# Layer 0: GpSimd joins the pair sums of sizes in twos, and TensorE sums once for four key tiles

## What is computed

```python
q = rotate(xn @ Wq.T); k = rotate(xn @ Wk.T * 32 ** -0.5); v = xn @ Wv.T      # xn: group norm of x
qk = einsum('bhqd,bhkd->bhqk', q, k) * mask[None]                              # decay by distance
den = clip(abs(qk).sum(-1, keepdims=True), 1.0, 50000.0)
out = einsum('bhqk,bhkd->bhqd', qk / den, v)
out = gelu((out - mean) / sqrt(var + 1e-5) * ln_g + ln_b) @ Wo.T;  x = x + out
```

## Time and profile before

| | us |
|---|---|
| median of 3 runs | 3395.98 (3387.21 to 3409.24) |
| the profiled execution, its span | 3401.5 |
| TensorE busy, whole span | 3075.4 |
| VectorE busy | 2193.4 |
| ScalarE busy | 2038.7 |
| GpSimd busy | 1165.8 |

### The profile page before, as it was taken

The page is one execution under the profiler, slowest core; times in us unless marked ns, Lnnn a source line. Parts: engine busy times, 40 slices in busy tenths (PEclk is TensorE's granted clock), DMA queues, the critical chain, the costliest instruction groups (busy, mean ns, idle before and its releaser), DMA issues. The chain is left out here.

```text
span 3401.5 us, 94014 instructions
## 1 busy us (share of the span) xinstructions
PE 3075.4 (90%) x38656; PEld 1731.0 (51%) x38656; DVE 2193.4 (64%) x5202; ACT 2038.7 (60%) x4412; POOL 1165.8 (34%) x1446
## 2 busy tenths in 40 slices
PE   6999999999975999999999877999995889999996
PEld 2333333333313656565555545777774566666664
DVE  5878878877753667767676643554554566666664
ACT  2667666766653555555655524566663677777774
POOL 3433434433311222122122202222222465555554
PEclk9999999999996999999999988999998999999998
DMA  6777788687763333233332214445444233333332
GB/s 203 159 173 158 164 178 182 140 184 160 150 141 107 67 88 78 67 82 80 85 73 76 73 41 163 141 149 163 148 134 154 62 93 115 112 117 114 114 98 80
DMA packets 299401, 413.96 MB, mean 122 GB/s; under 512 B 39120, under 2 KB 255968, under 8 KB 277984
## 3 DMA queue, kind: packets, MB, share of 16 engines
q1 hardware_dynamic: 275664, 272.15, 26.8%
q0 software_dynamic: 18432, 134.23, 19.8%
q10 hardware_dynamic: 4880, 1.57, 0.2%
HBM read 219.32 MB, written 53.81 MB: 80 GB/s over the span
## 5 line engine op out<-in xcount | busy, mean ns | idle before, releaser
L732 DVE TENSOR_TENSOR l_probs<-l_psum,l_decay 128x1024 f32<-128x1024 f32 x512 | 598.5, 1218 | 162.0 <-PE l_psum L628 149.6
L780 ACT ACTIVATE l_sizes<-l_probs 128x2048 f32<-128x2048 f32 x256 | 487.0, 1908 | 296.7 <-DVE l_probs L732 291.4
L1806 ACT ACTIVATE l_logits<-l_logits,l_low 128x100 f32<-128x100 f32 x1024 | 372.7, 366 | 205.9 <-DVE l_low L1786 205.0
L1813 POOL TENSOR_TENSOR l_logits<-l_logits,l_inv 128x400 f32<-128x400 f32 x256 | 234.7, 917 | 691.0 <-DVE l_inv L1792 686.6
L628 PE MATMUL l_psum<-l_qk 32*128 32x512 f32 x2048 | 338.4, 641 | 7.9 <-POOL l_qk L866 4.2
L881 POOL DMA_DIRECT2D l_sizes<-l_sizes x128 | 111.2, 869 | 548.1 <-ACT l_sizes L780 536.1
L1643 POOL TENSOR_TENSOR l_E<-l_E,l_causal 128x1024 f32<-128x1024 f32 x64 | 153.0, 2391 | 389.9 <-DVE l_x_act L1341 233.2
L643 PE MATMUL l_psum<-l_probs,l_V 128*32 128x512 f32 x2048 | 270.6, 600 | 1.8 <-DVE l_probs L732 1.6
L2753 POOL TENSOR_SCALAR l_soft<-l_dist,l_sharp,l_border 128x100 f32<-128x100 f32 x512 | 243.6, 497 | 0.1
L299 PE MATMUL l_psum<-l_xT,l_w_up 128*128 128x512 f32 x512 | 230.4, 603 | 13.2 <-DVE l_row_var L1399 13.1
L1748 PE MATMUL l_psum<-l_keys,l_q_blocks 128*64 128x100 f32 x4096 | 230.0, 253 | 3.9 <-issue 2.3
(11 more groups left out here) (247 smaller groups left out, 6085.1 us busy)
## 6 DMA issues: line engine op xcount, KB each, us to landing
l_sizes<-l_sizes POOLq DMA_DIRECT2D x128, 1024.0 KB, 7.5
l_V_windows<-v_image SPq DMA_DIRECT2D x512, 100.0 KB
l_V_windows<-v_padded SPq DMA_DIRECT2D x512, 100.0 KB
l_E<-rows_c SPq DMA_DIRECT2D x64, 512.0 KB, 5.9
l_xT<-y SPq DMA_DIRECT2D x24, 1024.0 KB, 5.2
y<-l_res SPq DMA_DIRECT2D x32, 512.0 KB, 3.2
l_e_everywhere<-rows_e SPq DMA_DIRECT2D x112, 128.0 KB, 5.7
l_xT<-x SPq DMA_DIRECT2D x8, 1024.0 KB, 10.8
```

The lines of the kernel that those rows point to most:

```text
L732: nc.vector.tensor_tensor(probs[:, N % 2, 2 * p:2 * p + 2, :], ring.region(name).rearrange("p (a n) -> p a n", a=2), decay[:, h:h + 2, s0: ...
L780: nc.scalar.activation(sizes[:, slot(N), :, :], probs[:, N % 2, :, :], ACT.Abs).then_inc(sized, 1)
L1806: nc.scalar.activation(e, e, ACT.Exp, scale=-1.0, bias=self.low[:, N % 4, i:i + 1], accum_out=self.total[:, N % 4, i:i + 1]).then_inc(self ...
L1813: nc.gpsimd.tensor_tensor(p, p, self.inv[:, N % 4, :].unsqueeze(2).to_broadcast([P, STEP, NKEY]), ALU.mult).then_inc(self.p_ready, 1)
```

## The change

Sizes are still added in pairs by transfers, but GpSimd now adds two pair sums into one (`join_pairs(f)`, a 128 x 2048 addition, f = N // 4), and TensorE sums once for each four steps: 64 groups of four products instead of 128. The sum of f stands after scores(4f + 8). `sizes` has six buffers instead of five (four for even steps, two for odd), and `swapped`, which the rotation uses, one instead of two. A join stands on GpSimd behind the add_pair of step 4f + 5, that is at n = 1, 5, 9 and 13. The fills now stand at the same steps for both g: q at 3, var at 5, k at 7, v at 11; `out` and `gn` stay. GpSimd's rotations stand at 3 and 7, `normalise` at 7, `inverse` at 6, `gelu` at 8, `values` at 11; the group norm's variance stays at 9 and its `apply` goes to 11. Line numbers of the new kernel are two or three lower (L650 is the sum, L878 the transfer, L884 the join).

```diff
@@ layer0_fill
-    late = 2 * g
-    names = {1 + late: [("q", H + 1)], 3 + late: [("k", H + 1)], 5 + late: [("var", H - 1)], 7 + late: [("v", H + 1)]}.get(n, [])
+    names = {3: [("q", H + 1)], 5: [("var", H - 1)], 7: [("k", H + 1)], 11: [("v", H + 1)]}.get(n, [])
...
-        sw = L.sb("swapped", [P, 2, T])
+        sw = L.sb("swapped", [P, T])
...
-        sizes = L.sb("sizes", [P, 5, 4, BANK])
+        sizes = L.sb("sizes", [P, 6, 4, BANK])
...
-            return N // 2 % 3 if N % 2 == 0 else 3 + N // 2 % 2
+            return N // 2 % 4 if N % 2 == 0 else 4 + N // 2 % 2
...
@@ TensorE
-                def add_sizes(p):
-                    pair_added(pe, p)
-                    if p % PAIRS == 0 and p > 0:
-                        pe.wait_ge(d_copied, p // PAIRS)
+                def add_sizes(f):
+                    pe.wait_ge(joined, f + 1)
+                    if f % FOURS == 0 and f > 0:
+                        pe.wait_ge(d_copied, f // FOURS)
                     for a in range(4):
-                        i = nc.tensor.matmul(PS[a * HD:(a + 1) * HD, 7 * BANK:8 * BANK], ones[:, :], sizes[:, slot(2 * p), a, :],
-                                             start=(p % PAIRS == 0), stop=(p % PAIRS == PAIRS - 1))
+                        i = nc.tensor.matmul(PS[a * HD:(a + 1) * HD, 7 * BANK:8 * BANK], ones[:, :], sizes[:, slot(4 * f + 2), a, :],
+                                             start=(f % FOURS == 0), stop=(f % FOURS == FOURS - 1))
...
-                        if n % 2 == 0 and N // 2 >= LATE:
-                            add_sizes(N // 2 - LATE)
+                        if n % 4 == 0 and N >= 8:
+                            add_sizes(N // 4 - 2)
...
@@ VectorE
-                    if U >= 2:
-                        dve.wait_ge(rot_done, U - 1)
+                    if U >= 1:
+                        dve.wait_ge(rot_done, U)
...
-                        if H > 0 and n == 7 + 2 * g:
+                        if H > 0 and n == 7:
                             normalise(H - 1)
...
@@ ScalarE
-                    if N % 2 == 0 and p >= 3:
-                        act.wait_ge(summed, p - 2)
+                    if N % 2 == 0 and p >= 4:
+                        act.wait_ge(summed if p % 2 else joined, (p - 4) // 2 + 1)
...
-                        if n == 6 + 2 * g and H > 0:
+                        if n == 6 and H > 0:
                             inverse(H - 1)
-                        if n == 7 + 2 * g and H + 1 < HALF_BATCHES:
+                        if n == 11 and H + 1 < HALF_BATCHES:
                             values(H + 1)
-                        if n == 8 + 2 * g and H > 0:
+                        if n == 8 and H > 0:
                             gelu(H - 1)
...
@@ GpSimd
                 def apply(b):
-                    norm.variance(nc, pool, pstep, ring, b)
                     pool.wait_ge(norm.got_root, b + 1)
...
+                def join_pairs(f):
+                    for p in (2 * f, 2 * f + 1):
+                        pair_added(pool, p)
+                    nc.gpsimd.tensor_tensor(sizes[:, slot(4 * f + 2), :, :], sizes[:, slot(4 * f + 2), :, :], sizes[:, slot(4 * f), :, :],
+                                            ALU.add).then_inc(joined, 1)
...
+                        p = H * QUADS // 2 + n // 2
                         if n % 2:
-                            add_pair(H * QUADS // 2 + n // 2)
-                        if n - 2 * g in (1, 3) and H + 1 < HALF_BATCHES:
-                            rotate(("q" if n - 2 * g == 1 else "k", H + 1))
+                            add_pair(p)
+                            if p % 2 == 0 and p > 0:
+                                join_pairs(p // 2 - 1)
+                        if n in (3, 7) and H + 1 < HALF_BATCHES:
+                            rotate(("q" if n == 3 else "k", H + 1))
                         if g == 0 and b + 1 < B and n == 9:
+                            norm.variance(nc, pool, pstep, ring, b + 1)
+                        if g == 0 and b + 1 < B and n == 11:
                             apply(b + 1)
+                join_pairs(HALF_BATCHES * QUADS // 4 - 1)
```

More of the change, by code:

```diff
@@ L493, in layer0 @@
         xn_ready, sw_ready, rot_done = L.sem("xn_ready"), L.sem("sw_ready"), L.sem("rot_done")
-        sized, weighed, summed = L.sem("sized"), L.sem("weighed"), L.sem("summed")
+        sized, weighed, joined, summed = L.sem("sized"), L.sem("weighed"), L.sem("joined"), L.sem("summed")
         o_copied, d_copied, den_ready = L.sem("o_copied"), L.sem("d_copied"), L.sem("den_ready")
@@ L549, in halved @@
             return k // 2 % HALVES, slice(k % 2 * BANK, (k % 2 + 1) * BANK)
-        PAIRS = NT // 2
-        LATE = 3
+        FOURS = NT // 4
         with nc.Block() as block:
@@ L669, in _ @@
                 weigh(last - 1)
-                for p in range(last // 2 - LATE, last // 2):
-                    add_sizes(p)
+                for f in range(last // 4 - 2, last // 4):
+                    add_sizes(f)
                 fill(("var", HALF_BATCHES - 1))
@@ L691, in rotate @@
                         s = slice(a * BANK, (a + 1) * BANK)
-                        nc.vector.stream_shuffle(sw[:, U % 2, s], ring.region(name)[:, s], [p ^ 1 for p in range(32)]).then_inc(sw_ready, 1)
+                        nc.vector.stream_shuffle(sw[:, s], ring.region(name)[:, s], [p ^ 1 for p in range(32)]).then_inc(sw_ready, 1)
                         i = nc.vector.tensor_tensor(by_row(qk[:, H % HALVES, U % 2, s]), by_row(ring.region(name)[:, s]),
@@ L790, in copy_sums @@
                     g, s = halved(k)
-                    act.wait_ge(summed, (k + 1) * PAIRS)
+                    act.wait_ge(summed, (k + 1) * FOURS)
                     nc.scalar.activation(D[:, g, s], PS[:, 7 * BANK:8 * BANK], ACT.Copy).then_inc(d_copied, 1)
@@ L861, in rotate @@
                         s = slice(a * BANK, (a + 1) * BANK)
-                        i = nc.gpsimd.tensor_tensor(by_row(sw[:, U % 2, s]), by_row(sw[:, U % 2, s]), turned(1, a), ALU.mult)
+                        i = nc.gpsimd.tensor_tensor(by_row(sw[:, s]), by_row(sw[:, s]), turned(1, a), ALU.mult)
                     pstep(pool, i)
@@ L865, in rotate @@
                     to = qk[:, g, U % 2, :]
-                    i = nc.gpsimd.tensor_tensor(to, to, sw[:, U % 2, :], ALU.add)
+                    i = nc.gpsimd.tensor_tensor(to, to, sw[:, :], ALU.add)
                     if name[0] == "q":
@@ L882, in add_pair @@
                                         accum_op=ALU.add).then_inc(added[p % 3], 16)
+                def join_pairs(f):
[3 more added lines that the diff above has]
+                                            ALU.add).then_inc(joined, 1)
+                norm.variance(nc, pool, pstep, ring, 0)
                 apply(0)
```

## The result

The changed kernel takes 3537.68 us (median, 3517.87 to 3549.05), before 3400.18 in the same runs: a ratio of 1.0385, 95% interval 1.0345 to 1.0426. The profiled execution lies at the low end of these. The page of the changed kernel: the span, the engines, then the costliest groups (busy us, mean ns of one, idle time before and its releaser).

A forecast was written before the change was run, and what follows sets the result against it. TensorE was taken to set the pace, VectorE right behind. 129.1 us per two half-batches instead of 118.8 led to 74 us, plus 14 for the clock, on 3401.5: 3489.5, as a median 3484; range 3390 to 3555.

The forecast's parts named there:

- The wait at step 5: VectorE's variance waits for GpSimd's denominator behind q's rotation; loss per two half-batches 3.3 us plus 0.5 (g = 1), 7.6 (g = 0).
- The joins: GpSimd's additions, 4.74 us each, make sums late: losses 1.7 and 3.3 us (g = 1), 1.0 and 2.5 (g = 0).
- The rival of hidden joins: Joins nearer 2.4 us, or covered by TensorE's delay at step 5, cost nothing: 3413 us, no change; chance 0.22.
- The sum: In layer 0, 109.2 us without new waits plus all losses: 129.1 us per two half-batches, 10.3 more than now.
- The clock: TensorE's granted clock falls behind long stops, 1.7 us of work lost each; one per image charged, 14 us in total.
- the first two: Of five long stops per image (2.1, 2.9, 1.7, 3.3, 2.5 us), those of 2.1 and 2.9, TensorE's at step 5.
- the rival in which all stops pay: All five long stops per image lose clock, so 14 us becomes 68: 3538 us; chance 0.14.
- No contention: VectorE's weights stay at 1210 to 1226 ns beside GpSimd's work, so nothing was charged for engines slowing each other.
- The saving: TensorE drops 64 groups of 0.85 us; with no new waits, two half-batches take 109.2 us, 9.6 below now.
- The plain reading: Also called Faster: TensorE is the bound and loses 64 x 0.85 = 54 us, giving 3342 us; chance 0.12.
- No effect: A rival: the removed sums lie in waits, so the time stays; no chance of its own was given.
- `swapped` at nothing: The single rotation buffer costs nothing, as k's rotation at 7 starts 6 us after q's has ended.

The follow-up runs named there:

- e3: The changed kernel with the fill var at step 6 instead of 5: 3484.9 us, ratio 1.0223 to the kernel before.
- e2: The kernel before, sums still in pairs, with only fills, rotations, normalise, inverse, gelu and values moved as in the change: 3448.8 us, ratio 1.0121.
- e4: The changed kernel with the join on one head of four (128 x 512, other heads' sums incomplete): 3453.6 us, ratio 1.0135 to the kernel before.
- e8: The changed kernel with 44 groups of overwritten products added where TensorE stood, at steps 0 and 7: 3493.9 us, ratio 1.0270 to the kernel before.
- e14: The changed kernel with one-head joins, var at 6, group norm's variance before the join, normalise before VectorE's reads of k: 3382.6 us, ratio 0.9929 to before.
- e10: The kernel before with only the single swapped buffer instead of two: 3409.0 us, ratio 1.0010.

## Why the prediction came out as it did

The direction was right, and most of the sum; the clock was mis-sized and one effect missing.

- **The wait at step 5.** `variance` waited 3.2 us each in 14 half-batches (44.4 of the 64.5; "about 3"), TensorE 2.5 with g = 0 (2.9) and 1.6 with g = 1 (2.1). e3 and e2 show that it costs.
- **The joins.** 4769 ns each against the 4.74 us taken from L866 doubled. The Trainium skill, "GPSIMD Engine Reference", section 3.1, has 4497 ns, which these rows reach only at their shortest (4484). The stops were 3.00 at n = 0 (3.3), 0.83 at n = 12 of g = 0 (1.0), 1.99 at v (2.5), and at n = 12 of g = 1 under 0.7 or 1.1 to 1.5 (1.7). The rival of hidden joins fell: their price is worth 85 us (e4).
- **The sum.** Six periods of after, from the sum at n = 0 with g = 0 to the next such, take 132.2 to 137.6 us, mean 135.3. The sum's 129.1 has no clock in it and no long `normalise`; e8, with no long `normalise` and a third of the half clock, has a mean of 129.6, and the stretch behind the step-5 wait of g = 0 takes 36.1 (35.9). The agreement is partly luck: it starts from 109.2, and even e14, where TensorE is busy 774 of 790 us (150 to 940), needs 116.0; and n = 0 to 4 of g = 1 took 22.5 in half-batch 9, where VectorE waited 6.11 us for the residual's transfer, which the working did not have.
- **The clock.** This step failed: "Behind the first two VectorE sets the pace and hides it; I take one per image, 14." It held for g = 0 and not for g = 1. The granted clock fell 29 times, behind most stops (0.51 from 603.4 to 606.8, behind that at step 5). At n = 0 it cost some 2.65 us where it fell for 5.4 us or more (the working had 1.7), and with g = 1 it fell for 6.8 us in steps 4 to 12 of six half-batches. In the profiled executions layer 0 lost 128 us where the working had 74 + 14 = 88. e8 gives 40 of these back and still loses 88: the miss is the clock and the long `normalise` together. The forecast of 3484 misses by 54; the rest lies between one execution and the median, and one profile cannot place it. That the rival in which all stops pay names 3538 is luck: two stops of 3.0 us at n = 0 lowered no clock, those of g = 0 at step 5 cost next to nothing, and that rival has no long `normalise`.
- **No contention.** "VectorE's weights stay at 1210 to 1226 ns whatever GpSimd does beside them, so I charge nothing for contention" was right for the weights (1206 to 1226 in after), wrong as a rule for all of VectorE. The first part says that the engines meet only at semaphores; VectorE and GpSimd met here without one. The weights read PSUM and SBUF, `normalise` reads two operands from SBUF. In after 7 of its 16 take 2.2 to 3.9 us, some 15 more in all; in before none met GpSimd. The change moved k's rotation to `normalise`'s step, and the working followed who waits for whom by semaphore alone.
- **The saving.** It is real, but small: with short joins, var at 6, the group norm's variance first and `normalise` moved, e14 is 0.7% faster, 24 of 54 us, at a clock of 1.00. Why no more is not shown; VectorE stood right behind TensorE, as the prediction said.
- The plain reading (*Faster*) and *No effect* are out by the result. `swapped` at nothing was right alone (e10).

## What to carry to other kernels

Work taken off a full engine and given to an idle one must be priced by when its result is ready, in the receiving engine's queue, not by its busy time: 54 us were to be saved, 305 were put on GpSimd, and the joins also held up what stood behind them (the chain to v, 1.99). Where a full TensorE begins to have stops of 1.5 to 3 us, count the work behind each stop at half clock unless another engine sets the pace there. An instruction that is moved must be looked at beside what the other engines then run, not only beside what it waits for.

## What the runs showed of the hardware

- In layer 0 of after TensorE stood 1.5 us or longer in 31 places. Behind 25 of them, and behind four stops of 1.2 to 1.4, the granted clock fell to the lower of its two levels, 1.2 instead of 2.4 GHz, for 3.4 or 6.8 us; two stops of 3.0 us were among the six that it did not follow. Overwritten products in the stops made the program faster by about 40 us, though they are 37 us of work (e8), in part because `normalise` then met GpSimd no more.
- VectorE's product of two SBUF operands can stand still while GpSimd runs an instruction: 1.23 us became 4.20 beside two rotations. In the traces of all fourteen kernels 63 of 224 `normalise` are long; each of these ran beside GpSimd and ended 1.1 us behind an instruction of it. Another 55 began ahead of GpSimd's instruction, 54 of them by 0.49 us or more, and kept to 1.2 us. The delay goes the other way as well: GpSimd's addition behind it, 2337 to 2384 ns for its kind, took 3.22 in this row of after (the `normalise` ran from 339.53 to 343.28).

```profile
342.26 3.22 POOL L863 TENSOR_TENSOR l_qk<-l_qk,l_swapped 128x1024 f32<-128x1024 f32 x1
```

The Trainium skill, "SBUF — State Buffer", section "SBUF: two separate sides", says that VectorE with two SBUF inputs and a GpSimd instruction that reads SBUF share one pair of ports, which the one that starts first holds until its end. The rows agree on the standing still, on weights that read PSUM being free of it, and on the 55 that were not held up. That VectorE waited for two GpSimd instructions in a row, and stood though its row begins up to 0.47 us ahead of GpSimd's (371.56 and 372.02 above), is more than the page says.
